# Self attention scores from single-pass fp32 parts, two heads above each other in the TensorE array

## The reference

```
def sdpa(q, k, v):                                  # per head, dh = 16
    scores = jnp.einsum('bid,bjd->bij', q, k) * 64 ** -0.5
    probs = jax.nn.softmax(scores, axis=2)
    return jnp.einsum('bij,bjd->bid', probs, v)

x = attention(ln32(x, ..), ln32(x, ..), Wq1, Wkv1, Wo1, bo1) + x    # self: 1024 x 1024 scores a head
x = attention(ln32(x, ..), context, Wq2, Wkv2, Wo2, bo2) + x        # 1024 x 154 scores a head
x = geglu_ff(ln32(x, ..), Wff1, bff1, Wff2, bff2) + x
x = softmax_attention_of_one_head(x, context, L1 weights) + x
```

## Time and profile before

| | us |
|---|---|
| median of 3 runs | 1642.72 |
| span of the profiled execution | 1641.9 |
| first to last maximum matmul | 46.7 to 1449.8 |
| PE busy | 1557.9 (95%) |
| DVE busy | 1103.1 (67%) |
| ACT busy | 995.2 (61%) |
| POOL busy | 252.9 (15%) |

### The profile page before, as it was taken

One profiled execution on the slowest core, in us unless ns is written; L12 is line 12 of the kernel. 1 busy time (PEld: TensorE's weight loads), 2 busy tenths in 40 slices (PEclk: granted clock), 3 DMA queues, 4 the chain that ended last, 5 costly groups with the idle time before them and its releaser, 6 DMA issues.

```text
span 1641.9 us, 33969 instructions
## 1 busy us (share of the span) xinstructions
PE 1557.9 (95%) x12833; PEld 1011.8 (62%) x12833; DVE 1103.1 (67%) x2269; ACT 995.2 (61%) x2024; POOL 252.9 (15%) x342
## 2 busy tenths in 40 slices
PE   6899999999999999999999999999999999998887
PEld 5454545675757666675767667565656656574766
DVE  4667776858676776858677686858677675843433
ACT  4365667666667566666657566666656555664342
POOL 1210412111112021111112021010011010101110
PEclk9999999999999999999999999999999989997999
DMA  9914242555231412645131321356121311303210
GB/s 236 206 39 139 69 71 83 103 108 109 63 84 46 82 51 72 113 98 119 58 86 47 70 58 58 80 98 116 44 73 35 71 42 44 82 31 73 56 34 13
DMA packets 177116, 129.76 MB, mean 79 GB/s; under 512 B 40975, under 2 KB 168889, under 8 KB 176697
## 3 DMA queue, kind: packets, MB, share of 16 engines
q1 hardware_dynamic: 176889, 127.58, 33.0%
q10 hardware_dynamic: 64, 0.02, 0.0%
HBM read 79.24 MB, written 47.71 MB: 77 GB/s over the span
## 4 chain that ended last, share of the span: by engine, by line
PE 71%; DVE 14%; DMA 7%; ACT 3%; SPq 2%; issue 2%; POOL 0%; DVEq 0%; ACTq 0%; POOLq 0%
PE ps_o L1709 11%; PE ps_max L1679 10%; PE ps_last L1622 10%; PE ps_s L1697 9%; PE ps_last L1631 6%; DVE mxh L1360 6%; PE ps_pre L1486 4%; PE ps_cross L1590 4%; DVE mx L1286 3%; PE ps_pre L1494 3%; PE ps_cross L1576 3%; DMA o_s<-den_c 2%; DMA den<-o_s 2%; PE ps_last L1644 1%; PE ps_last L1659 1%
## 5 line engine op out<-in xcount | busy, mean ns | idle before, releaser
L1360 DVE TENSOR_REDUCE mxh<-ps_max 128x1 f32<-128x512 f32 x1024 | 655.8, 683 | 175.2 <-PE ps_max L1679 173.3
L1143 ACT ACTIVATE probs<-ps_s 128x512 f32<-128x512 f32 x1024 | 579.4, 597 | 232.2 <-PE ps_s L1697 185.4
L1679 PE MATMUL ps_max<-kst,qst 96*128 96x512 bf16 x1024 | 371.5, 386 | 22.0 <-DVE mxh L1360 14.7
L1697 PE MATMUL ps_s<-qst,kst 98*128 98x256 bf16 x2048 | 368.2, 275 | 6.1 <-ACT probs L1143 4.3
L1697 PEld LDWEIGHTS ps_s<-qst,kst 98*128 98x128 bf16 x2048 | 178.8, 98 | 146.6 <-ACT probs L1143 49.4
L1709 PE MATMUL ps_o<-probs,vg 128*17 128x256 f32 x4096 | 268.4, 384 | 0.0
L1679 PEld LDWEIGHTS ps_max<-kst,qst 96*128 96x128 bf16 x1024 | 96.0, 97 | 146.5 <-DVE mxh L1360 91.2
L1087 ACT ACTIVATE probs<-ps_cross 77x512 f32<-77x512 f32 x224 | 132.7, 592 | 78.1 <-PE ps_cross L1576 77.2
L1318 DVE SCALAR_TENSOR_TENSOR th<-th,gb 128x256 f32<-128x256 f32 x128 | 56.9, 445 | 164.3 <-ACT gb L1118 164.3
L1709 PEld LDWEIGHTS ps_o<-probs,vg 128*17 128x17 f32 x4096 | 96.5, 97 | 110.4 <-issue 49.8
L1622 PE MATMUL ps_last<-y_hi,wff_hi 128*128 128x256 f32 x448 | 139.6, 312 | 4.8 <-DVE y_lo L1312 2.5
(11 more groups left out here) (261 smaller groups left out, 1951.7 us busy)
## 6 DMA issues: line engine op xcount, KB each, us to landing
parts_s<-qk_parts SPq DMA_DIRECT2D x28, 384.0 KB, 4.3
o_s<-o_sb SPq DMA_DIRECT2D x64, 128.0 KB, 2.6
o_s<-o_sb SPq DMA_DIRECT2D x32, 256.0 KB, 2.2
oT<-o_s SPq DMA_DIRECT2D x62, 128.0 KB
den<-o_s SPq DMA_DIRECT2D x62, 128.0 KB
q_s<-qk_parts SPq DMA_DIRECT2D x16, 384.0 KB, 2.3
q2st<-q_s SPq DMA_DIRECT2D x16, 384.0 KB, 5.3
q2st<-q_s SPq DMA_DIRECT2D x48, 128.0 KB, 6.1
```

The lines of the kernel that those rows point to most:

```text
L1143: nc.scalar.activation(probs[:, step % PR, 2 * pair:2 * pair + 2, :].rearrange("p j q -> p (j q)"), ps_s[pair][:, :], ACT.Exp, scale=SCALE ...
L1360: nc.vector.tensor_reduce(mxh[:, i % PAIRS, i // PAIRS:i // PAIRS + 1], ps_max[i % 2][:, :], AX_X, ALU.max).then_inc(g_mx, 1)
L1679: mm(ps_max[i % 2][:, :], qst[0:ROWS, h, q * P:(q + 1) * P], kst[0:ROWS, h, half * 512:(half + 1) * 512], start=True, stop=True).then_inc( ...
L1697: last = mm(ps_s[pair][:, j * CH:(j + 1) * CH], kst[:, h, kt * P:(kt + 1) * P], qst[:, h, :], start=True, stop=True)
```

## The change

**Parts.** q and k are split in two float32r parts (a rounded one and the rest), in tiles of 4 bytes; the middle part is gone, and with it one POOL copy and one POOL subtraction a tensor, and in the first four chunks one ACT cast (L978) and one DVE subtraction (L1190) a tensor. A head's stack has 48 rows (3 x 16) of 4 bytes, so as many bytes as before; 50 with the maxima. `parts_s` holds 8 bytes for each element of q or k, where it held 6.

**Two heads above each other.** `qst` and `kst` hold the even head of a pair at partitions 0 and the odd one at partition 64. A letter M with even k now issues both tiles k and k+1, one for each head, at `tile_position` (0, 0) and (64, 0), into both banks of `ps_max`; odd ones issue nothing on PE. A letter S with even k issues four matmuls: two heads by two blocks of keys, into both banks of `ps_s`. The numbers of letters, and the order on DVE and ACT, stay. A tile of S is now one head by two blocks of keys, so the exponential writes two pieces of `probs`, and a V letter's first half also waits for all four exponentials.

```diff
+HP = H // 2
+ROW_TILE = P // 2
+SELF_ROWS = 3 * DH
-        qst = sb("qst", [ROWS + SHIFT, H, CH], BF16)
-        kst = sb("kst", [ROWS + SHIFT, H, S], BF16)
+        qst = sb("qst", [P, HP, CH], F32R)
+        kst = sb("kst", [P, HP, S], F32R)
@@ sync: store_shift
-                for row_, part in ((ROWS, sh_hi), (ROWS + 1, sh_lo)):
-                    sp.dma_start(qst[row_:row_ + 1, heads, :].rearrange("a j (q p) -> a (j q) p", p=P),
-                                 part[:, :]).then_inc(g_shl, 16)
+                for e in range(2):
+                    for i, part in enumerate((sh_hi, sh_lo)):
+                        row_ = e * ROW_TILE + SELF_ROWS + i
+                        sp.dma_start(qst_w[row_:row_ + 1, pairs, :].rearrange("a j (q p) -> a (j q) p", p=P),
+                                     part[e * PAIRS // 2:(e + 1) * PAIRS // 2, :].bitcast(F32)).then_inc(g_shl, 16)
@@ gpsimd: pre
-                    parts(qk_f[i], qk_parts[i], PART_AT[i], a_f[i], a_hi[i], a_rest[i], a_mid[i], a_lo[i], p + 1,
-                          p - MAX_LAG + 1)
+                    nc.gpsimd.tensor_tensor(lo, lo.bitcast(F32), hi.bitcast(F32), ALU.subtract).then_inc(a_lo[i], 1)
@@ scalar: exp_tile
-                step, pair = divmod(k, 2)
-                act.wait_ge(g_s, 2 * step + pair + 1)
+                j, step = k % G, k // G * 2
+                act.wait_ge(g_s, k + 1)
                 if step >= PR:
-                    act.wait_ge(g_av, step - PR + 1)
-                nc.scalar.activation(probs[:, step % PR, 2 * pair:2 * pair + 2, :].rearrange("p j q -> p (j q)"),
-                                     ps_s[pair][:, :], ACT.Exp, scale=SCALE).then_inc(g_e, 1)
+                    act.wait_ge(g_av, step + 2 - PR)
+                nc.scalar.activation(probs[:, step % PR:step % PR + 2, j, :], ps_s[k % 2][:, :].rearrange(
+                    "p (a q) -> p a q", a=2), ACT.Exp, scale=SCALE).then_inc(g_e, 1)
@@ tensor: max_scores
+                if i % 2:
+                    return
-                pe.wait_ge(g_mx, unit * 2 * PAIRS + max(0, i - 1))
-                mm(ps_max[i % 2][:, :], qst[0:ROWS, h, q * P:(q + 1) * P],
-                   kst[0:ROWS, h, half * 512:(half + 1) * 512], start=True, stop=True).then_inc(g_mt, 1)
+                pe.wait_ge(g_mx, k)
+                for e in range(2):
+                    rows = slice(e * ROW_TILE, e * ROW_TILE + SELF_ROWS)
+                    mm(ps_max[e][:, :], qst[rows, at, q * P:(q + 1) * P], kst[rows, at, half * 512:(half + 1) * 512],
+                       start=True, stop=True, tile_position=(e * ROW_TILE, 0)).then_inc(g_mt, 1)
@@ tensor: scores
+                if i % 2:
+                    return
-                pe.wait_ge(g_e, max(0, 2 * step + pair - 1))
-                for j in range(2):
-                    h = unit % HG * G + 2 * pair + j
-                    last = mm(ps_s[pair][:, j * CH:(j + 1) * CH], kst[:, h, kt * P:(kt + 1) * P],
-                              qst[:, h, :], start=True, stop=True)
-                last.then_inc(g_s, 1)
+                pe.wait_ge(g_e, k)
+                for a in range(2):
+                    for e in range(2):
+                        rows = slice(e * ROW_TILE, e * ROW_TILE + SELF_ROWS + SHIFT)
+                        last = mm(ps_s[e][:, a * CH:(a + 1) * CH], kst[rows, at, (kt + a) * P:(kt + a + 1) * P], qst[rows, at, :],
+                                  start=True, stop=True, tile_position=(e * ROW_TILE, 0))
+                        if a == 1:
+                            last.then_inc(g_s, 1)
@@ tensor: values_of
-                pe.wait_ge(g_e, 2 * step + 2)
+                pe.wait_ge(g_e, (step // 2 + 1) * G)
```

More of the change, by code:

```diff
@@ L230, in xattn_kernel @@
         pre_yT = sb("pre_yT", [P, KD, CH])
-        qk_parts = [sb(f"qk_parts{i}", [P, 3, KD * CH], BF16) for i in range(2)]
-        qk_f = [sb(f"qk_f{i}", [P, KD * CH]) for i in range(2)]
+        qk_parts = [sb(f"qk_parts{i}", [P, 2, KD * CH], F32R) for i in range(2)]
         v_sb = sb("v_sb", [P, TT, H, VW])
@@ L974, in head @@
                             wait_parts(act, p - 1)
-                        nc.scalar.copy(parts[i][:, PART_AT[i][0], :], ps_s[i][:, :]).then_inc(a_hi[i], 1)
-                    for i in range(2):
-                        act.wait_ge(a_rest[i], p + 1)
-                        nc.scalar.copy(parts[i][:, PART_AT[i][1], :], xf[i][:, :]).then_inc(a_mid[i], 1)
+                        nc.scalar.copy(parts[i][:, SELF_AT[i][0], :], ps_s[i][:, :]).then_inc(a_hi[i], 1)
                     if p >= 2:
@@ L1359, in max_half @@
                 dve.wait_ge(g_mt, k + 1)
-                nc.vector.tensor_reduce(mxh[:, i % PAIRS, i // PAIRS:i // PAIRS + 1], ps_max[i % 2][:, :], AX_X,
-                                        ALU.max).then_inc(g_mx, 1)
+                half, pair = i // PAIRS, i % 2 * PAIRS // 2 + i % PAIRS // 2
+                nc.vector.tensor_reduce(mxh[:, pair, half:half + 1], ps_max[i % 2][:, :], AX_X, ALU.max).then_inc(g_mx, 1)
             def max_pairs(unit):
@@ L1666, in max_scores @@
                 unit, i = divmod(k, 2 * PAIRS)
+                if i % 2:
+                    return
                 c, g = divmod(unit, HG)
-                pair, half = i % PAIRS, i // PAIRS
-                h, q = g * G + pair // TT, pair % TT
+                half, at, q = i // PAIRS, g * G // 2 + i % PAIRS // 4, i % PAIRS // 2 % TT
                 if i == 0:
@@ L1686, in scores @@
             def scores(k):
-                step, pair = divmod(k, 2)
-                unit, kt = divmod(step, KT)
+                unit, i = divmod(k, 2 * KT)
+                if i % 2:
+                    return
+                at, kt = unit % HG * G // 2 + i // 2 % 2, i // 4 * 2
                 if k == 0:
```

123 lines of the change are left out of this document (65 added, 58 removed).

## The result

Three runs of the changed kernel gave 2081.51, 2081.73 and 2089.11 us, median **2081.73 us**, against 1642.72 before: a ratio of 1.269, 95% interval 1.265 to 1.273. It is slower, as forecast, but by 439 us and not by 117. The range ended at 1877. In what follows the M, S and V matmuls are L1690, L1711 and L1724, the reduction is L1369, the exponential L1153.

A forecast was written before the change was run, and what follows sets the result against it. PE was taken as the bound. In the maximum stretch 1234 us of work plus 290 of waits made 1524 against 1403, so +121; with -3 at the head, 1641.9 became 1760 us, range 1630 to 1877.

The forecast's parts named there:

- PE's work: Matmul time on PE in the maximum stretch: 208 us saved by pairs, 164 added by shape changes, 1278 to 1234.
- rival C: Row pairs on PE do not run at once, or their weight loads follow one another: 1877 us, chance 14%.
- B: Rival: changes to row pairs on PE are free and weights come early: 1651 us, 1625 to 1695, chance 17%.
- M loop: Even maximum tiles on PE wait for DVE's reductions of both banks: 1.86 us a turn, 213 us of waiting.
- S loop: Score tiles on PE wait for ACT's two exponentials: 1.65 us a turn, 37 us taken, bounds 0 and 74.
- The second half of V's wait was the same before: V letter's wait on PE, listed among the edits that cost nothing.
- The clock: PE's granted clock in the stretch: taken as 0.99, nothing to win or lose; a drop named as possible error, unpriced.
- 4-byte weight loads after waits: Weight loads on PE held back with a wait: 0.09 us more in each turn of the maximum loop.
- others: Waits of PE at letters other than maxima and scores: 52 us before, 40 kept, bounds 0 and 52.
- Rival A: Waits of PE stay as they are, 125 us: 1595 us; faster under 169 us of waiting; chance 14%.

The follow-up runs named there:

- the first three runs: Kernel before, tiles issued in twos: 1937 us. Changed kernel, one tile at a time with waits of before: 1843 us. Changed kernel, full array: 2068 us.
- the even order: Row form, one tile at a time, M and S letters rewritten side by side at even distances: 2374 us; score tile from the other 64 rows: 2170 us.

## Why the prediction was wrong

- **PE's work (forecast 1234, found 1192 us).** Right in kind. Pairs run at once, so rival C falls; changes of shape cost, so B falls: the step from scores into V is 0.21 us, 0.12 of matmul and 0.09 of change, and the step from L1584's full-array matmul to a pair of maxima 0.20, where to one maximum before it was 0.11. So a change into a row pair is 0.09 and not the 0.20 of the forecast; but out of a pair of maxima, for which I had 0.10, it is 0.20 (0.42 to L1584 for 0.22 of work), and the two together are 0.29 where I had 0.30. By the same measure the work before is 1263 us, or 1283 with the small excesses, where I had 1278; the saving is 71 to 91 us, not 44. The Trainium skill, TensorEngine Tiling (Array Packing), section Key Properties, has a change of mode drain TensorE; the steps agree, now for rows too, by 0.09 us. The Trainium skill, TensorE: Matmul & The Clock Gate, Part 3, has tiles in different row groups run some 4 ns apart; the records' 0 to 4 ns agree.
- **M loop (213, found 181 us, or 131 with whole letters as steps).** Right: the mechanism and the 1.86 us (1.88); the sum was somewhat too large. The summation over the order with DVE's other work put in worked.
- **S loop (37, found 205 us, or 151 with whole letters as steps): the first step that failed.** I took one turn as 0.51 + 1.08 + 0.06 = 1.65 us "taken after the waits at M", and between 0 and 74 us in all. I put DVE's other work into the M loop but the S loop as written has none of ACT's: 127 of the 236 places hold some, and the turn is 2.88 us on average. Bf16 scores in twos alone cost 147 us.
- **V, left out of the S loop.** I wrote "The second half of V's wait was the same before", priced it at nothing, and did not ask who waits for V. The exponentials do, V stands behind the scores on PE, and with a wait for both banks that closes a circle: 99 us by the run that opened it. The edit itself was priced rightly, or nearly: on the kernel before, the new tile costs 12 us. The circle does not need it: in bf16 with the old tile the exponentials wait for V for 173 us with both in twos and for 123 us with the scores in twos, where the kernel before has 35. What had covered it was the spare bank, which the pairs took away. How much the new tile adds to it in the changed kernel, no run shows.
- **The clock (0.99 assumed, 0.86 granted; at most 189 us): the second step that failed.** I wrote "nothing to win or lose in it as long as PE stays this busy", gave 85% or less of PE's busy share as a sign of being right, named the clock as what might be wrong and still gave it no price. At its upper bound it is the largest term of the miss.
- **4-byte weight loads after waits.** Reckoned in the M loop and at changes of shape only; raw parts in the full array cost 67 us more than bf16 with the same tile, some 20 of them by the slower pass. In the table the loads stand partly in the waits ahead of S.
- **Sum of the miss.** In the stretch -42 (work) - 32 (M) + 168 (S) + 18 (others) + 189 (clock) = +301, and +19 outside it: 320 of the 322 us, by a division that depends on what is taken as a step, with the clock at its upper bound. By runs, each against the one before it: tile of one head +12, 4-byte parts +67, row form +122, pairs with double waits +239. That these add up to the measured 439 proves nothing, since each is the difference to the next; and the shares depend on the order, for in pairs the row form adds only 14 us and the pairs in the full array 347 (2068 - 1721).
- **Rival A, faster under 169 us of waiting,** was far away: 444.

What lowered the clock, four of the runs separate. Granted clock over the span, and us of the maximum stretch at the lower level:

| raw parts | one tile at a time | in pairs, waiting for both banks |
|---|---|---|
| full array | 0.982, 0 us | 0.927, 236 us |
| row form | 0.923, 242 us | 0.863, 522 us |

Pairs with double waits take 0.055 to 0.060, the row form 0.059 to 0.064, each with or without the other. The double waits do it in bf16 too (0.941 against 0.986 beside it), though not those of the scores alone (0.980). And the row form does it without leaving PE idle; the pages of the two one-tile kernels, full array and then row form:

```profile
PE 1628.2 (95%) x12833; PEld 1195.1 (70%) x12833; DVE 1110.0 (65%) x2261; ACT 995.9 (58%) x2016; POOL 212.0 (12%) x295
PE 1747.8 (95%) x12833; PEld 1128.2 (61%) x12833; DVE 1114.4 (61%) x2261; ACT 997.6 (54%) x2016; POOL 211.3 (11%) x295
```

PE's busy time holds modelled ends, but its idle times of over 0.15 us in the maximum stretch say the same: 26 us in the full array, 46 in row form and 304 in the changed kernel. So each of the two theories of the first three runs was half right. What in the row form does it, half of the rows or the 1073 more changes of shape, stays open, and the 189 us are an upper bound.

## What to carry to other kernels

Two tiles issued at once into both banks of a double buffer leave no buffer: the saving on PE must be set against a loop through the reader, with every other instruction of that reader counted in it, for each of the letters that do so. Where tiles can overlap, neighbours of different chains can do it without a new wait (a maximum beside a score, each waiting for its own bank): that was worth 204 us in the even order, between two kernels slower than all the others, and no run here shows it in a good one. Count the clock among the costs, and not only where PE waits: the row form lowered it from 0.982 to 0.923 with PE 95% busy in both. When a change takes the slack of one buffer, look again at each wait that was covered by it, and ask of each waiting instruction what on its releaser's engine stands in front of the releaser.

## What the runs showed of the hardware

The clock. Busy us of the changed kernel in two neighbouring windows (PE, PEld, DVE, ACT, POOL, granted clock):

```profile
999.50:1009.50 10.00, 6.95 (x79) 3.94 (x77) 9.06 (x20) 4.84 (x10) 3.97 (x6) 1.00 0.09 23
1009.50:1026.50 17.00, 14.06 (x79) 8.74 (x78) 7.64 (x19) 6.00 (x12) 0.93 (x2) 0.50 0.01 2
```

and a V letter in each:

```profile
1005.05 1.06 PE L1724 MATMUL ps_o<-probs,vg 128*17 128x256 f32 x16
...
1010.76 1.91 PE L1724 MATMUL ps_o<-probs,vg 128*17 128x256 f32 x16
```

In the first window, at 2.4 GHz, PE was busy for 6.95 of 10 us, with single idle times of up to 1.3 us; then the clock stood at 1.2 GHz for 17 us and the same 16 matmuls took 1.91 us, not 1.06. The changed kernel spent 522 us of the maximum stretch at this level, the kernel before 17. So many short waits can cost twice: once themselves and once in the pace of the work behind them (bf16 in twos: 0.941 against 0.986).

A change of shape costs about 0.09 us into four columns and about the same into row pairs (0.20 us from L1584 to a pair of maxima, 0.11 before to one). A weight load of 4 bytes and 128 columns adds about 0.1 us wherever the work ahead of it does not hide it: the second two score matmuls of a pair start 0.22 us behind the first two after L1630 or V, and 0.12 after maxima that did not wait.
